# A graph transformer layer with a 64-expert block on one core: graph layer by thirds, denominators turned in nine steps, final stage by pairs of tiles

## What is computed

```python
xn = _layernorm(x, axis=-1)
# graph attention, 8 heads of 32
att = jnp.exp(jnp.einsum('ehd,ehd->eh', Q[receivers], K[senders]) / sqrt(DK))
att = att / segment_sum(att, receivers, num_segments=N)[receivers]
agg = zeros.at[receivers].add(att[:, :, None] * V[senders])
gnn = relu(relu(relu(agg).reshape(N, 256) @ Wa + ba) @ Wf + bf)
x = x + (xn + gnn) + mix(xn)                       # mix: linear attention, 8 heads of 64
h = _ln(x, ln1_g, ln1_b)
vals, idx = top_k(softmax(h @ Wr @ codebook.T / TEMP), 2)     # weights w, 64 experts
moe = sum_k w_k * (silu(h @ W1[e_k] + b1[e_k]) @ W2[e_k] + b2[e_k])
shared = (silu(h @ Ws1 + bs1) @ Ws2 + bs2) * 0.25
hmoe = moe + shared
f = _ln(hmoe, ffln_g, ffln_b)
out = x + hmoe + (silu(f @ Wf1 + bf1) @ Wf2 + bf2)
```

## Time and profile before

| | us |
|---|---|
| median of 3 runs | 1026.12 |
| lowest, highest | 1025.73, 1027.83 |
| the profiled execution, its own time | 1019.11 |
| its span | 1017.4 |
| PE busy in it (89%) | 902.4 |
| DVE, ACT, POOL busy | 548.6, 278.5, 151.8 |

### The profile page before, as it was taken

How to read it: one execution, slowest core, us unless ns; L and a number is a source line. 1 busy time by engine, 2 the same in 40 slices (tenths; PEclk the granted TensorE clock), 3 DMA queues, 4 the chain that set the end, 5 groups by cost and what they waited for, 6 DMA issues and landing times.

```text
span 1017.4 us, 12227 instructions
## 1 busy us (share of the span) xinstructions
PE 902.4 (89%) x4038; PEld 485.2 (48%) x4038; DVE 548.6 (54%) x1352; ACT 278.5 (27%) x484; POOL 151.8 (15%) x190
## 2 busy tenths in 40 slices
PE   2899997999999999999897996999999999985278
PEld 1564444645683333333544773545645654442134
DVE  7785556666757999989167540222222222222872
ACT  2631110101126656665235410111211211111231
POOL 3000002200100000000002536122222222233000
PEclk9999999999999999999899998899999999997589
DMA  9200000001345214010016122488888887984412
GB/s 297 86 17 26 1 1 1 1 0 51 152 103 120 62 41 101 1 41 1 1 41 229 41 90 85 157 280 293 285 285 305 292 287 279 314 310 165 122 51 90
DMA packets 42107, 129.89 MB, mean 128 GB/s; under 512 B 9121, under 2 KB 9603, under 8 KB 41407
## 3 DMA queue, kind: packets, MB, share of 16 engines
q1 hardware_dynamic: 33019, 110.77, 33.8%
q0 software_dynamic: 8576, 18.03, 5.1%
q10 hardware_dynamic: 452, 0.34, 0.1%
HBM read 118.52 MB, written 19.71 MB: 136 GB/s over the span
## 4 chain that ended last, share of the span: by engine, by line
PE 62%; DVE 16%; issue 6%; DVEq 4%; DMA 4%; POOL 4%; ACT 3%; SPq 1%; ACTq 0%; POOLq 0%; PEldq 0%; PEld 0%
PE ps L1327 7%; PE ps L1544 6%; PE ps L1465 5%; PE ps L1562 5%; DVE att L872 5%; PE ps L1477 5%; PE ps L1354 3%; PE ps L1363 3%; PE ps L1410 3%; PE ps L1309 3%; PE ps L1295 2%; DVE rden L856 2%; POOL list_d L570 2%; PE ps L1399 2%; PE ps L1428 2%
## 5 line engine op out<-in xcount | busy, mean ns | idle before, releaser
L872 DVE TENSOR_TENSOR att<-ps,C 125x832 f32<-125x832 f32 (+1 forms) x120 | 118.3, 1003 | 18.1 <-ACT ps L1154 15.9
L1154 ACT ACTIVATE ps<-ps 125x832 f32<-125x832 f32 (+1 forms) x120 | 101.7, 849 | 68.0 <-PE ps L1399 67.0
L1410 PE MATMUL ps<-att,V 125*64 125x416 f32 (+1 forms) x480 | 110.4, 538 | 5.2 <-DVE att L872 5.1
L1005 DVE TENSOR_SCALAR hgT<-ps,cols 128x128 f32<-128x128 f32 x148 | 50.4, 403 | 85.1 <-PE ps L1531 84.7
L1011 DVE COPY ehT<-ps 128x256 f32<-128x256 f32 x36 | 15.3, 425 | 118.4 <-PE ps L1552 118.4
L1399 PE MATMUL ps<-Qst,Kst 128*125 128x416 f32 (+1 forms) x240 | 76.7, 401 | 2.1 <-DVE C L846 0.7
L1477 PE MATMUL ps<-Ws_s,hsT 128*125 128x512 f32 x160 | 73.6, 598 | 0.0
L1544 PE MATMUL ps<-W,hgT 128*64 128x256 f32 x576 | 73.3, 399 | 0.0
L1465 PE MATMUL ps<-hT,Ws_s 128*128 128x250 f32 x320 | 72.4, 381 | 1.0 <-ACT combT L1210 1.0
L1399 PEld LDWEIGHTS ps<-Qst,Kst 128*125 128x125 f32 x240 | 35.3, 185 | 79.6 <-DVE att L872 42.5
L1327 PE MATMUL ps<-mW,xnT 128*125 128x512 f32 x160 | 72.2, 594 | 0.0
(11 more groups left out here) (234 smaller groups left out, 1270.7 us busy)
## 6 DMA issues: line engine op xcount, KB each, us to landing
W<-in_W SPq DMA_DIRECT2D x144, 512.0 KB
Kst<-qk_d SPq DMA_DIRECT2D x32, 156.2 KB, 5.7
Qst<-qk_d SPq DMA_DIRECT2D x32, 156.2 KB, 5.9
Yt<-y_d SPq DMA_DIRECT2D x10, 448.0 KB
Ws_s<-in_Ws SPq DMA_DIRECT2D x2, 2048.0 KB, 14.2
qk_d<-qk_hi POOLq DMA_DIRECT2D x4, 625.0 KB, 3.6
qk_d<-qk_lo POOLq DMA_DIRECT2D x4, 625.0 KB, 4.5
z_d<-yz POOLq DMA_DIRECT2D x10, 250.0 KB, 2.7
```

Of the source, the lines that this page charges most:

```text
L872: V_.tensor_tensor(att[:, n % 3, :, 0:w], scores_of(n, w), C[:, s, o:o + w].unsqueeze(1).to_broadcast([P, 2, w]), ALU.mult).then_inc(att_m ...
L1005: i = V_.tensor_scalar(hgT[:, u, k, :], bank(u, 128, 128, k * 128), col("g1", k), col("b1ln", k), ALU.mult, ALU.add)
L1154: S_.activation(b, b, ACT.Exp, scale=float(DK) ** -0.5).then_inc(s_exp, 1)
L1410: k = MM(sums_of(i, 64 * j, 64, w), V[:, s, pair, j:j + 2, :], att[:, n % 3, j, 0:w], start=s == 0, stop=s == T - 1, skip_group_check=True)
```

## The change

The diff is cut to what matters below; what it does, by stage:

- **Attention.** The thirds are now 416, 416 and 418. PE's drain and ACT's `keep_den` are gone. `keep_heads` has nine steps, all on DVE and beside the multiplies of the next set: two transposes in blocks of 32x32 straight from PSUM (after which each denominator stands once, every 32nd column), the tiny constant and the reciprocal on 128x13, two transposes back with a repeated source, four products of 32x208.
- **Graph layer.** `gnn_a` goes chunk by chunk and `gnn_f` of a chunk's tiles follows it. The first chunk waits for the set before the last only.
- **Shared parts.** Hidden pieces 10 and 11 move ahead of the first expert pair, shared tiles 8 and 9 behind the last. Ahead of the first pair there are also eight one-column multiplies of Wf1 with the bias `bfln` (`fb`), and DVE multiplies Wf1 by the gain `gf` while the pairs run.
- **Final stage.** `Yt` has eight buffers, so the loads of the first eight tiles wait for nothing. All goes by pairs of tiles; the normalising moves from DVE to ACT, the reading of the transposed tiles to ACT alone, as one plain copy for a tile, and `f1` goes by 250 columns. The ten adds of `HM` to `XR` move from DVE to POOL. `shared_sum` of tiles 8 and 9 stands among DVE's pairs.

```diff
-THIRDS = [(0, 418), (418, 416), (834, 416)]
-WIDE = 418
+THIRDS = [(0, 416), (416, 416), (832, 418)]
+WIDE = 448
...
+    parts = ([("shared", t, k) for t in (2, 3) for k in range(3)]
              + [("hidden", i, k) for i in range(12, 16) for k in range(2)] + [("shared", t, k) for t in (4, 5) for k in range(3)]
-             + [("hidden", i, k) for i in range(16, 20) for k in range(2)] + [("shared", t, k) for t in range(6, 10) for k in range(3)])
+             + [("hidden", i, k) for i in range(16, 20) for k in range(2)] + [("shared", t, k) for t in (6, 7) for k in range(3)])
...
-                if t >= 2:
-                    sp.wait_ge(yt_used, t - 1)
+                if t >= YB:
+                    sp.wait_ge(yt_used, t - YB + 1)
...
+            for t in range(T):
+                gp.wait_ge(yt_used, t + 1)
+                nc.gpsimd.tensor_tensor(XR[:, t, :], XR[:, t, :], HM[:, t, :], ALU.add).then_inc(xs_made, 1)
...
-                if step < 4:
-                    c = slice(step * w // 4, (step + 1) * w // 4)
-                    V_.reciprocal(rden[:, c], rden[:, c])
...
+                if step < 2:
+                    if step == 0:
+                        v.wait_ge(att_used, T * i + T)
+                    c = slice(224 * step, (224, w32)[step])
+                    V_.transpose(sumsT[:, c], sums_of(i, 0, 128, w32)[:, c])
+                elif step == 2:
                     v.drain()
+                    V_.tensor_scalar(dens[:, 0:w32 // 32], sumsT[:, 0:w32:32], TINY, None, ALU.add)
+                    v.drain()
+                    V_.reciprocal(dens[:, 0:w32 // 32], dens[:, 0:w32 // 32])
...
-                if i >= 1 and 1 <= s <= 6:
+                if i >= 1 and s >= 1:
                     keep_heads(i - 1, s - 1)
...
+            for k in range(KD):
+                V_.tensor_scalar(Wf1_s[:, k, :], Wf1_s[:, k, :], col("gf", k), None, ALU.mult)
+            v.drain().then_inc(f1_folded, 1)
...
+            for c in range(T // 2):
+                if c in (1, 2):
+                    shared_sum(7 + c)
+                weighed(c, 0)
+                if c:
+                    scales(c - 1)
+                weighed(c, 1)
+                stats(HM, mv, (2 * c, 2 * c + 1), f_var)
+                if c == 3:
+                    for t in range(2):
+                        output(t)
+            scales(T // 2 - 1)
+            for t in range(2, T):
+                output(t)
...
+            def normed(t):
+                if t % 2 == 0:
+                    a.wait_ge(rz_made, t // 2 + 1)
+                if t >= 4:
+                    a.wait_ge(filled, TURNS.filled("fT", t - 4))
+                S_.activation(fz[:, t % 4, :], HM[:, t, :], ACT.Identity, bias=nb[:, t:t + 1], scale=rs[:, t:t + 1]).then_inc(fz_made, 1)
...
+            stds(0)
+            stds(1)
+            normed_pair(0)
+            f_read_pair(0)
+            stds(2)
+            normed_pair(1)
+            f_read_pair(1)
+            normed_pair(2)
+            f1_read(0)
...
-                if s == T - 1:
-                    pe.drain().then_inc(head_sum, 1)
...
-            pe.wait_ge(head_kept, SETS)
+            pe.wait_ge(head_kept, SETS - 1)
...
+            for c, (o, n) in enumerate(CHUNKS):
+                if c == 1:
+                    pe.wait_ge(head_kept, SETS)
...
+            for i in range(8, 12):
+                whole_hidden(i)
+            pe.wait_ge(wf1_in, 16)
+            b = turn("fb", 0)
...
             result(2 * H + 1, H, 1)
+            for t in (8, 9):
+                for third in range(3):
+                    shared_rows(t, third)
```

More of the change, by code:

```diff
@@ L95 @@
 ]), (6, 0, [
-    ("gnn_a", ["act"] * 12),
-    ("gnn_f", ["dve"] * 10),
+    ("gnn_a", ["act"] * 4), ("gnn_f", ["dve"] * 4),
+    ("gnn_a", ["act"] * 4), ("gnn_f", ["dve"] * 4),
+    ("gnn_a", ["act"] * 4), ("gnn_f", ["dve"] * 2),
     ("hT", ["act", "dve"] * 5),
@@ L497, in _ @@
             nc.gpsimd.memset(eps2[:, :], 1e-10)
-            nc.gpsimd.memset(tiny[:, :], TINY)
             gp.drain()
@@ L1065, in _, with weighed, scales @@
-            for i in range(4, T):
-                output(i)
+            def weighed(c, k):
+                for t in (2 * c, 2 * c + 1):
+                    if k == 0:
+                        v.wait_ge(yt_in[t % YB], 16 * len(PARTS) * (t // YB + 1))
+                    i = V_.scalar_tensor_tensor(HM[:, t, :], Yt[:, t % YB, k, :], wtop[:, t, k:k + 1], HM[:, t, :], ALU.mult, ALU.add)
+                    if k == 1:
+                        i.then_inc(yt_used, 1)
+                v.drain()
+            def scales(c):
+                p = slice(2 * c, 2 * c + 2)
+                v.wait_ge(f_std, c + 1)
+                V_.reciprocal(rs[:, p], rs[:, p])
+                v.drain()
+                V_.scalar_tensor_tensor(nb[:, p], mv[:, p, 0], -1.0, rs[:, p], ALU.mult, ALU.mult)
+                v.drain().then_inc(rz_made, 1)
@@ L1429, in _ @@
                     i.then_inc(filled, 1)
-            read_by_now("gnn_a", 11)
-            for t in range(T):
-                b = turn("gnn_f", t)
-                for k in range(KD):
-                    i = MM(bank(b, D, P), h1T[:, k, t * P:t * P + P], Wf_s[:, k, :], start=k == 0, stop=k == KD - 1)
-                i.then_inc(filled, 1)
+                for t in range(o // P, (o + n) // P):
+                    b = turn("gnn_f", t)
+                    for k in range(KD):
+                        if t == o // P:
+                            read_by_now("gnn_a", KD * c + k)
+                        i = MM(bank(b, D, P), h1T[:, k, t * P:t * P + P], Wf_s[:, k, :], start=k == 0, stop=k == KD - 1)
+                    i.then_inc(filled, 1)
             for t in range(T):
@@ L1594, in _, with f_transposed @@
             pe.wait_ge(e_read, 2 * H + 2)
-            def f_transposed(tiles):
-                for t in tiles:
+            def f_transposed(c):
+                for t in (2 * c, 2 * c + 1):
                     pe.wait_ge(fz_made, t + 1)
```

229 lines of the change are left out of this document (115 added, 114 removed).

## The result

The changed kernel takes 995.14 us (median of 4 runs, 990.90 to 997.54), against 1025.92 for the kernel before (4 runs). The ratio is 0.9699, with a 95% interval of 0.9666 to 0.9733: some 31 us faster, where 42.7 were forecast. 995 lies inside the stated range of 970 to 997, near its slow end.

A forecast was written before the change was run, and what follows sets the result against it. PE was taken to bound the kernel nearly everywhere, with DVE sharing the attention. Terms -6.6 - 7.6 - 1.4 - 13.4 - 13.7 = -42.7, taken off the median 1026.1, gave 983.4 us (chance 0.49), range 970 to 997.

The forecast's parts named there:

- Attention, -6.6: Attention: drain and DVE backlog vanish, transposes at the copy's 0.4 us; 0.60 us a set over eleven sets, -6.6 us.
- (e): Attention: transposes run at the reciprocal's rate, 1.5 us each, +20.5 in place of -6.6, total 1010.5 us; chance 0.04.
- (f): Attention: transposes dearer still, kernel slower than before from 1.85 us a transpose, 1037 at 2.1 us; chance 0.02.
- Graph layer, -7.6: Graph layer: PE starts chunk 0 without waiting and stays warm, gnn_f ends at 536.7; -7.6 us (-5 to -8.5).
- Start of the pairs, -1.4: Ahead of the first pair: hidden pieces and one-column products fill PE's 8.76 us hole; -1.4 us (-2.7 to +1).
- PE comes warm: Start of the pairs: PE reaches the transposes at full clock, so they and the multiplies behind run faster; 2.7 us back.
- Loop, -13.4: Expert pairs: moved shared work saves 20.2 us, gather waits grow from 0.7 to about 7; -13.4 us (0 to -20).
- (b): Expert pairs: the loop doesn't wait at all, the shown gather landing being a late one; total 976.4 us; chance 0.12.
- (d): Expert pairs: the loop gains nothing because transfers set its pace; total 996.8 us; chance 0.06.
- (a): Expert pairs: gathers slower by 1 us, waits grow from 7 to about 15.5 us; total 991.9 us; chance 0.17.
- Final stage, -13.7: Final stage: shared tiles fill PE's hole, PE ends at 999.8 against 1013.5; -13.7 us (-6 to -16).
- (c): Final stage: POOL's adds hold up DVE's multiplies, +3.7 us to 987.1, at most +12; chance 0.10.

The follow-up runs named there:

- f_only: The kernel before with only the new final stage (gain and bias folded into Wf1); attention, graph layer and shared parts as before: 1023.83 us, 0.9954 of before.
- u_shared: The changed kernel with hidden pieces 10 and 11 and shared tiles 8 and 9 put back beside the expert pairs: 1010.85 us, 0.9841 of before.
- f_counts: The changed kernel with PE's final-stage waits counting ACT's reads in the order ACT makes them, not the table's: 983.70 us, 0.9575 of before.

## Why the prediction was right or wrong

- **Attention, -6.6.** Mechanism and price right: a transpose at the copy's 0.4 us, backlog and drain gone, (e) and (f) out. Between 192 and 224 columns a transpose grows from 0.372 to 0.404 us, 1 ns a column, where the reciprocal has about 7. The Trainium skill's pipelined transpose of one element per cycle per lane (Vector Engine (DVE) Microarchitecture Reference, section 3.8, The reshape front-end and per-opcode configuration) goes with that rate, though no row here gives the length of a cycle. Measured -6.0 where PE starts warm in both. The -3.7 of the first trace sets a cold start against a warm one; the sum left out that PE can reach the stage before Q lands, which the old attention meets as well.
- **Graph layer, -7.6.** Right: -7.1.
- **Start of the pairs, -1.4.** Wrong in sign, +1.4 in the first trace and +0.8 in the second. The one-column products were cheaper than either bound, 0.12 us a record (1.93 for 16) against 0.16 to 0.22. The step that failed is "PE comes warm": in all eleven traces in which the hole is full the first hidden takes 3.6 to 3.7 us, in the first after waits of 0.40 and 0.49 us for the gathers, in the second after 0.25 and 0.23. Whether these short waits or the thin one-column products ahead of them are to blame is open; no run leaves either out. Beside this, the list came later: one of DVE's reads for the ranks waited 1.8 us for PE, 0.3 before.
- **Loop, -13.4.** Right: -13.3 and -12.7 up to the fourth-last transposes, waits of 6.6 us where 7 were forecast. Not all of them were for gathers, as the prediction had said: 0.9 us were for W1 and biases, a sign of being wrong by its own words, but small. The term for the tail, 0, can't be judged from one trace of before: 29.0 there, but 33.5 and 36.6 in the two kernels with the same pairs, 32.5 and 34.4 after. (b) and (d) are out by this; (a) too, since the waits did not double.
- **Final stage, -13.7.** Wrong: -1.6 and -3.7. The entry was right, 24.9 against 24.6 us. The step that failed is "waits for ACT ... I take 2.0 (none to 7)" and "a slow start ... 1.7". The waits ahead of f1 alone are 0.67 x 3 + 4.31 + 4.22 = 10.5, and cold f1 added 2.8 + 1.7 + 2.7 = 7.2 over 3.65. The prediction priced ACT's fixed order of work, but did not set it beside the table from which PE's counts are made. With the counts mended, 68.2 us against the 69.1 forecast.
- **POOL's adds, rival (c).** The mechanism is there, the price is not. Groups by form, after, then the two engines side by side:

```profile
L1074 DVE SCALAR_TENSOR_TENSOR HM<-Yt,wtop,HM 125x512 f32<-125x512 f32 x20 | 14.6, 764 | 13.5 <-DMA Yt<-y_d 12.7
L624 POOL TENSOR_TENSOR XR<-XR,HM 125x512 f32<-125x512 f32 x10 | 14.7, 1491 | 34.4 <-DVE HM L1074 34.4
```

```profile
935.48 0.75 DVE L1074 SCALAR_TENSOR_TENSOR HM<-Yt,wtop,HM 125x512 f32<-125x512 f32 x1
935.64 1.71 POOL L624 TENSOR_TENSOR XR<-XR,HM 125x512 f32<-125x512 f32 x1 [2.92 <-DVE HM L1074]
...
937.32 1.26 POOL L624 TENSOR_TENSOR XR<-XR,HM 125x512 f32<-125x512 f32 x1
...
938.04 1.09 DVE L1074 SCALAR_TENSOR_TENSOR HM<-Yt,wtop,HM 125x512 f32<-125x512 f32 x1
```

  The means, 764 and 1491 ns, mix two kinds. An add that starts 0.16 us after a multiply takes 1.70 to 1.72 us, five of the ten; the others take 1.26 to 1.28, as those of the earlier trace rows. The one multiply that starts while an add has 0.54 us to go takes 1.09; the other nineteen stay at 0.75. The one that came first is not slowed: the multiply at 935.48 takes 0.75, the add at 937.32 takes 1.26. The twelve other traces of the new final stage show the same, f_only and u_shared with three slow multiplies each, since no shared_sum stands between them there. So the Trainium skill's rule (SBUF — State Buffer, section Who interferes with whom), that the later of the two waits, agrees with the trace in kind. The later one lost somewhat less than the first had left to run: the add 0.45 of 0.58 us, the multiply 0.34 of 0.54, where (c) took a whole add for each of two or three multiplies. The forecast's "multiplies at 0.75" failed for one of twenty, and "1 us or more" was its sign of being wrong. It cost nothing on the way to the first f1, since that multiply stands behind it. What made the one long DVE operation of the earlier trace rows was not tested.
- **The sum.** The time is 11.7 us above the forecast and still inside the range. By the traces the stages miss theirs by 21.8 us in all: 12.1 in the final stage, 3.5 in the tail, 2.9 in the attention, 2.8 in the start, 0.5 in the rest. By the medians it is 11.9, because the profiled execution of before was 7 us below its median and that of after 2.4 above; how these 9 to 10 us fall on the stages is open. With the counts mended the kernel takes 983.70 us, the forecast's 983.4. The final stage's part of that agreement is shown; that the rest comes out to the microsecond is luck.

## What to carry to other kernels

Where semaphores count an engine's work by a table, the table's order must be that engine's program order. A mismatch makes one count too high, which shows as a wait whose releaser in the trace is an operation that the waiting one doesn't need; it makes another too low, which here did no harm only because a higher count had been waited for first. When a PE wait of 4 us stands in a stage, price the cold clock behind it as well: here two waits of 8.5 us together brought 4 to 5 more. A mean over a group can hide two kinds of instruction: look at the single ones that overlap before ruling a collision out. When one late transfer is mended, look for the next in the same loop before trusting the gain, and mend them together.

## What was not expected of the hardware

- After waits of 4.2 to 4.3 us in which PE did nothing, f1 took 5.1 to 6.4 us in place of 3.65; in f_counts, after 0.67 to 0.76, all but the first f1 held. At the attention's start waits of 1.5 to 2.1 us for Q went with first sums of 1.5 to 1.7 us in place of 0.92, waits of 0.2 to 0.4 us with 0.92.
- A multiply with one column costs 0.12 us a record beside 0.22 for 250 columns.
- The order in which SP issues weight loads of the same size and number changed how long POOL's gathers take to land, from 7.1 to 7.4 us to 5.8 (medians), and PE's waits for them from 5.7 to 2.6 us up to the fourth-last transposes, with the gathers issued as late as ever.
- POOL's adds and DVE's multiplies with two operands in SBUF held each other up by 0.3 to 0.5 us whenever one began while the other ran; the one that began first kept its time.
